# Moving the Newton part of the norm chains to GpSimd, loading the next expert's register earlier, and a new set of due times

## The reference

```
x = x + A(layernorm(x))          # A: linear attention, (theta phi^T) g / 16, no softmax
x = x + F(layernorm(x))          # F: a transformer layer of its own
F(x): h = rmsnorm(x) * ln1;  q, k, v = h @ wqkv   (16 query heads, 4 kv heads of 16), rope on q, k
      x = x + softmax(causal(q k^T / 4)) v @ wo
      h = rmsnorm(x) * ln2;  top 2 of 8 experts by softmax(h @ gate)
      out = sum over chosen experts of weight * (silu(h @ w1) * (h @ w3)) @ w2     (ffn 512)
      return x + out
```

## Time and profile before

| | us |
|---|---|
| median of 3 runs | 1060.29 (1058.63 to 1061.31) |
| the profiled execution, its time | 1058.78 |
| the profiled execution, its span | 1057.1 |
| PE busy | 1011.6 in 6264 instructions |
| DVE busy | 789.2 in 1701 |
| ACT busy | 661.5 in 1305 |
| POOL busy | 435.5 in 476 |
| PE matmuls of `warm` steps (L2046), part of PE busy | 27.5 |

### The profile page before, as it was taken

How to read it: one execution, slowest core, us unless ns; L and a number is a source line. 1 busy time by engine, 2 the same in 40 slices (tenths; PEclk the granted TensorE clock), 3 DMA queues, 4 the chain that set the end, 5 groups by cost and what they waited for, 6 DMA issues and landing times.

```text
span 1057.1 us, 19430 instructions
## 1 busy us (share of the span) xinstructions
PE 1011.6 (96%) x6264; PEld 594.6 (56%) x6264; DVE 789.2 (75%) x1701; ACT 661.5 (63%) x1305; POOL 435.5 (41%) x476
## 2 busy tenths in 40 slices
PE   5999999999999999999999999999989999999997
PEld 4765335443453333453334444456678888888886
DVE  5689979787778998899857997136776666666664
ACT  3562785747768878847767656684534555555553
POOL 1020145155732144422545325457477543444443
PEclk9999999999999999999999999999999999999999
DMA  6433114132336557732343412243434333222220
GB/s 200 128 123 103 53 46 143 55 115 77 97 109 194 146 188 212 203 95 82 111 120 109 137 25 70 52 92 82 103 78 98 73 57 52 48 47 46 48 46 11
DMA packets 86642, 102.33 MB, mean 97 GB/s; under 512 B 17904, under 2 KB 74224, under 8 KB 86544
## 3 DMA queue, kind: packets, MB, share of 16 engines
q1 hardware_dynamic: 72240, 81.46, 26.3%
q0 software_dynamic: 14304, 19.63, 10.1%
HBM read 56.22 MB, written 41.01 MB: 92 GB/s over the span
## 4 chain that ended last, share of the span: by engine, by line
PE 74%; DVE 16%; ACT 5%; issue 3%; DMA 1%; POOL 1%; DVEq 0%; ACTq 0%; POOLq 0%
PE psum L2171 10%; PE psum L2157 9%; PE psum L2209 6%; PE psum L2213 5%; PE psum L2137 5%; PE psum L2210 5%; DVE psum L1932 5%; PE psum L2211 5%; PE psum L2123 3%; PE psum L2219 3%; PE psum L2237 3%; PE psum L2140 2%; PE psum L2231 2%; PE psum L2233 2%; PE psum L2232 2%
## 5 line engine op out<-in xcount | busy, mean ns | idle before, releaser
L1440 ACT ACTIVATE probs_mem<-psum 128x512 f32<-128x512 f32 (+1 forms) x464 | 232.0, 584 | 90.2 <-PE psum L2157 89.0
L1932 DVE CUSTOM_DVE_ANT_1 psum<-psum,masking 128x640 f32<-128x640 f32 (+3 forms) x256 | 257.2, 1045 | 32.9 <-PE psum L2140 32.1
L1337 POOL DMA_INDIRECT out<-yout,labels x71 | 133.7, 1884 | 182.9 <-DMA out<-yout,labels 86.8
L2157 PE MATMUL psum<-stack_mem 98*128 98x512 bf16 (+3 forms) x768 | 169.3, 327 | 3.3 <-DVE mx L1932 1.8
L1292 POOL TENSOR_SCALAR_AFFINE_SELECT probs_mem<-probs_mem 128x512 f32<-128x512 f32 x104 | 66.9, 644 | 223.9 <-ACT probs_mem L1440 223.6
L2157 PEld LDWEIGHTS psum<-stack_mem 98*128 98x128 bf16 x768 | 64.6, 97 | 105.3 <-issue 21.9
L2171 PE MATMUL psum<-probs_mem,v 128*17 128x512 f32 (+3 forms) x1152 | 117.1, 490 | 0.8 <-POOL probs_mem L1292 0.5
L2015 DVE TENSOR_TENSOR w_lo<-w_mem,w_hi 128x1024 fp32r<-128x1024 f32 x51 | 62.5, 1225 | 65.5 <-PE psum L2233 57.3
L1934 DVE TENSOR_REDUCE mx<-psum 128x4 f32<-128x512 f32 (+2 forms) x96 | 96.1, 1036 | 13.1 <-PE psum L2145 10.8
L2137 PE MATMUL psum<-stack_mem 96*128 96x512 bf16 x256 | 95.2, 383 | 5.4 <-DVE mx L1932 2.6
L2209 PE MATMUL psum<-w_hi,x_hi 128*128 x216 | 93.6, 433 | 6.2 <-issue 2.4
(11 more groups left out here) (229 smaller groups left out, 2070.8 us busy)
## 6 DMA issues: line engine op xcount, KB each, us to landing
block<-routed SPq DMA_DIRECT2D x71, 129.0 KB, 2.5
w_mem<-in_w13T SPq DMA_DIRECT2D x16, 512.0 KB, 4.9
qk_parts<-w_mem SPq DMA_DIRECT2D x16, 384.0 KB, 2.9
stack_mem<-qk_parts SPq DMA_DIRECT2D x32, 192.0 KB, 3.3
w_mem<-in_x SPq DMA_DIRECT2D x8, 512.0 KB, 5.1
out<-w_mem SPq DMA_DIRECT2D x8, 512.0 KB, 4.0
x_late<-out SPq DMA_DIRECT2D x8, 512.0 KB, 5.0
stack_mem<-qk_parts SPq DMA_DIRECT2D x32, 128.0 KB, 2.7
```

The costliest lines, as they stand in the source:

```text
L1337: e.indirect_dma_start(out_rows, bass.IndirectOffsetOnAxis(ap=labels[w % NLABEL].bitcast(I32)[:, 0:1], axis=0), youts[w % NYOUT], None, bo ...
L1440: e.activation(probs[probs_of(m)][:, hh:hh + n, q0:CH], grid(turn[step][0][:, 0:n * (CH - q0)], n), ACT.Exp, scale=float(HD) ** -0.5).then ...
L1932: e.tensor_tensor_reduce(keys, keys, masked(w), 1.0, -3e38, ALU.add, ALU.max, to).then_inc(sem["max"], 1)
L2157: m = e.matmul(bk[:, i * (CH - q0):(i + 1) * (CH - q0)], s[0:STACK + NMAX, kt // TPR, GRP, kt % TPR * P:(kt % TPR + 1) * P], s[0:STACK + N ...
```

## The change

Three edits.

1. `rsqrt` is cut in two. The seed is now one DVE instruction in place of two. For batches 1 to 3 norm1 and norm2 stop after the seed on DVE (2 and 3 steps), and norm3 does so for all batches (2 steps); the Newton steps and what follows them run on POOL in chains of 15, 18 and 13 steps (`norm1_rest`, `norm2_rest`, `norm3_rest`). Batch 0's norm1 and norm2 stay on DVE whole. [...]
2. PE's load of the next block's register stands in the second half of the current block's `up`, behind the products of k = 0. The first block of each batch's list (w = 0, 9, 25, 41) still loads ahead of its first half.
3. The planner's costs for `label`, `w2_lo` and the norm steps, its constants `LIKE` and `AHEAD`, and the whole table `NUDGE` are new.

```
-RSQRT_STEPS = 11
+RSQRT_STEPS = 10
-NORM1_STEPS, NORM2_STEPS, NORM3_STEPS = RSQRT_STEPS + 2, RSQRT_STEPS + 5, RSQRT_STEPS + 1
+NORM1_STEPS, NORM2_STEPS, NORM3_STEPS = RSQRT_STEPS + 2, RSQRT_STEPS + 5, 15
+NORM1_SEED, NORM2_SEED, NORM3_SEED = 2, 3, 2
+NORM1_REST, NORM2_REST, NORM3_REST = 15, 18, 13
-TURN, LIKE = 0.1, (3.1, 0.06)
+TURN, LIKE = 0.1, (2.5, 0.05)
-AHEAD = {"DVE": 1.7, "ACT": 1.9}
+AHEAD = {"DVE": 1.9, "ACT": 1.8}
 NUDGE = {
-        "aggr": {(0,): -126.5},
+        "aggr": {(1,): 1.2, (2,): 24.8},
...
+            def newton(name, dst, a, u, w):
+                in_chain(name)
+                e.tensor_scalar(a, a, -0.5, None, ALU.mult).then_inc(sem[name], 1)
+                yield
+                for _ in range(3):
+                    in_chain(name)
+                    e.tensor_tensor(u, dst, dst, ALU.mult).then_inc(sem[name], 1)
+                    yield
+                    in_chain(name)
+                    e.tensor_tensor(w, u, a, ALU.mult).then_inc(sem[name], 1)
+                    yield
+                    in_chain(name)
+                    e.tensor_scalar(w, w, 1.5, None, ALU.add).then_inc(sem[name], 1)
+                    yield
+                    in_chain(name)
+                    e.tensor_tensor(dst, dst, w, ALU.mult).then_inc(sem[name], 1)
+                    yield
...
                 elif stage == "h2":
-                    q.wait_ge("norm3", NORM3_STEPS * (b + 1))
+                    q.wait_ge("norm3_rest", NORM3_REST * (b + 1))
...
-                e.tensor_scalar(ui, ai, 1, None, ALU.logical_shift_right).then_inc(sem[name], 1)
-                yield
-                in_chain(name)
-                e.tensor_scalar(di, ui, -1.0, float(0x5F3759DF), ALU.mult, ALU.add).then_inc(sem[name], 1)
+                e.tensor_scalar(dst.bitcast(I32), a.bitcast(I32), -0.5, float(0x5F3759DF), ALU.mult, ALU.add).then_inc(sem[name], 1)
...
                 elif stage == "gate":
-                    q.wait_ge("norm3", NORM3_STEPS * (b + 1))
+                    q.wait_ge("norm3_rest", NORM3_REST * (b + 1))
...
-                    if half == 0:
+                    if half == 0 and w not in offset:
...
                             m = e.matmul(bk, blockT[w % 2][:, k], w13_s[:, k, of], start=first, stop=final)
+                        if half == 1 and first and (gi, c + 1) in WORK:
+                            offset[w + 1] = e.value_load(bexp[gi][0:1, c + 1:c + 2], min_val=0, max_val=(NE - 1) * 2 * FFN)
```

More of the change, by code:

```diff
@@ L246, in work_of @@
         return ("PE", 1.38 if at[0] >= DOWN_FROM else 1.73), ("ACT", 0.37), ("POOL", 1.6)
+    if stage in ("norm1", "norm2", "norm3"):
+        seed = {"norm1": NORM1_SEED, "norm2": NORM2_SEED, "norm3": NORM3_SEED}[stage]
+        return (("POOL", 0.2),) if at[1] >= seed and (at[0] or stage == "norm3") else (("DVE", 0.08),)
     if stage == "w13_lo":
@@ L288 @@
+        "split": {(3,): 9.6},
+        "spread": {(3,): 6.6},
+        "square": {(1,): 0.7},
+        "square_sum": {(2,): -9.6},
+        "stats": {(3,): 5.8},
+        "stats2": {(1,): 9.4, (2,): 0.3},
+        "theta": {(2,): 55.7, (3,): -46.6},
+        "v": {(1,): -9, (2,): -90.5, (3,): -1.2},
+        "w13": {(): -75.5},
+        "weight": {(0,): 48},
+        "wo": {(2,): -37.3},
+        "x1": {(2,): -5.4},
+        "xn": {(1,): 23.3},
+        "xnT": {(1,): -0.5, (3,): -1.2},
 }
@@ L377, in needs @@
         if stage == "norm2":
-            return [("aggr2", b, (TPB if b else HALF * (at[1] // NORM2_STEPS + 1)) - 1)] + [(stage, b, at[1] - 1)] * (at[1] > 0) + [(stage, b - 1, norm_parts(b - 1) * NORM2_STEPS - 1)] * (b > 0 and not at[1])
+            return [("aggr2", b, (TPB if b else HALF * (at[1] // NORM2_STEPS + 1)) - 1)] + [(stage, b, at[1] - 1)] * (at[1] > 0) + [(stage, b - 1, norm_parts(b - 1) * norm_steps("norm2", b - 1) - 1)] * (b > 0 and not at[1])
         if stage == "h":
-            return [("norm2", b, (1 if b else at[1] // HALF + 1) * NORM2_STEPS - 1)] + in_order(step)
+            return [("norm2", b, (1 if b else at[1] // HALF + 1) * norm_steps("norm2", b) - 1)] + in_order(step)
         if stage == "hT":
@@ L538, in project @@
                 continue
-            steps += [(half, ("norm1", b, i)) for i in one_part(b, half, NORM1_STEPS)] + [(half, ("xn", b, j)) for j in (range(TPB) if b else tiles)]
+            steps += [(half, ("norm1", b, i)) for i in one_part(b, half, norm_steps("norm1", b))] + [(half, ("xn", b, j)) for j in (range(TPB) if b else tiles)]
         steps += [(2, ("gram", b, i)) for i in range(gram_steps(b))] + [(2, ("square", b, i)) for i in range(2)]
@@ L548, in project @@
                 continue
-            steps += [(6 + half, ("norm2", b, i)) for i in one_part(b, half, NORM2_STEPS)]
+            steps += [(6 + half, ("norm2", b, i)) for i in one_part(b, half, norm_steps("norm2", b))]
             for at in range(2) if b else (half,):
@@ L948, in mega_kernel, with normed @@
         routing = [carve(route_mem, route_sizes)] * len(GROUPS)
+        def normed(stage, b, n):
+            if b < 1:
+                return stage, {"norm1": NORM1_STEPS, "norm2": NORM2_STEPS}[stage] * n * (b == 0)
+            return f"{stage}_rest", {"norm1": NORM1_REST, "norm2": NORM2_REST}[stage] * b
         def masked(w):
@@ L1269, in _, with norm3_rest, go_on @@
+            def norm3_rest(b):
+                q.wait_ge("norm3", NORM3_SEED * (b + 1))
+                t = rt[:, 2]
+                yield from newton("norm3_rest", rstd2, t[:, 1], t[:, 2], t[:, 3])
+            def go_on(make, b):
+                if (make, b) not in chains:
+                    chains[make, b] = make(b)
+                next(chains[make, b])
             for step in orders["POOL"]:
                 stage, *at = step
-                if stage == "split":
+                if stage == "norm1":
+                    go_on(norm1_rest, at[0])
+                elif stage == "norm2":
+                    go_on(norm2_rest, at[0])
+                elif stage == "norm3":
+                    go_on(norm3_rest, at[0])
+                elif stage == "split":
@@ L1567, in norm2 @@
                     yield
-                    yield from rsqrt("norm2", scale, s[:, 0:2], s[:, 2:4], s[:, 4:6])
+                    seed("norm2", scale, s[:, 0:2])
+                    yield
+                    if b:
+                        return
+                    yield from newton("norm2", scale, s[:, 0:2], s[:, 2:4], s[:, 4:6])
                     in_chain("norm2")
@@ L1583, in norm3 @@
                 q.wait_ge("h2", TPB * b)
+                q.wait_ge("norm3_rest", NORM3_REST * b)
                 t = rt[:, 2]
@@ L1587, in norm3 @@
                 yield
-                yield from rsqrt("norm3", rstd2, t[:, 1], t[:, 2], t[:, 3])
+                seed("norm3", rstd2, t[:, 1])
+                yield
             def route(gi):
```

116 lines of the change are left out of this document (78 added, 38 removed), and 2 rows, old and new, of the table WORK_OF.

## The result

The changed kernel takes 1042.05 us, the median of four runs (1039.46 to 1044.08), against 1059.6 for the kernel before beside it. The ratio is 0.983, with a 95% interval of 0.981 to 0.986. The forecast was 1044.

A forecast was written before the change was run, and what follows sets the result against it. Up to 800 us PE had 62 us of slack; after that PE or its sequencer bound the kernel. 9 (load, last stage) + 2 (earlier blocks) + 5 (chains, order) = 16 us off 1058.78, plus 1.5: 1044, range 1031 to 1056.

The forecast's parts named there:

- the largest term: Last stage, from 800 us on: moving the register load off the block border gains 9 us.
- the last step of the sum: Whole kernel: the median lies 1.5 us above the profiled execution, turning 1042.8 into 1044.3 us.
- The last stage: 9 forecast: Expert blocks from w = 23 on: 9 us gained, the middle of 11.5 by PE and 6.4 by the adds.
- a lead of 1.5 us: Second half of `up`: PE's sequencer is 1.5 us ahead, covering some 0.6 us of load, so it costs nothing.
- PE's 11.5: Last stage by PE alone: 46 moved loads at 0.25 us each gain 11.5 us.
- the adds' 6.4: Last stage if an add into `out` takes 5.03 us each: 46 x 0.14 = 6.4 us gained.
- an upper figure of the adds' period: Adds into `out`: 5.03 us each is above a free-running chain's floor, since issues take 1.56 to 2.16 us.
- The chains and the order with the blocks up to w = 22: 7 forecast: Stretch up to 800 us: shorter by some 7 us, 2 from blocks w = 13 to 22 and 5 from chains and order.
- The 5 us for chains and order: Norm chains and new order together: 5 us, half of 9.3 us of removed filler; possibly nothing, minus 6 or 15.
- The rival of late chains: Norm chains queue on POOL, steps 0.8 us, `h` 10 to 12 us late: 1073, slower than before; chance 0.10.
- The signs: Marks of being right: no PEld idle at block starts, period 4.9 to 5.05 us, DVE down 20, POOL up 30.

The follow-up runs named there:

- the kernel with less PE work: The changed kernel without the product w_lo x x_hi in `up` from w = 23 on, so part of the result is missing: 1027.79 us (0.970).
- the later copy: The changed kernel with the copy of batch 3's second routing weights moved behind the w_lo of down(22) in DVE's queue: 1039.24 us (0.979).
- the old due times and the order kept: The load-only kernel with the Newton parts run on POOL where DVE's steps stood in planner time, all other orders kept: 1054.36 us (0.995).
- with the old due times a part of it did: The changed kernel with the old NUDGE, LIKE, AHEAD and costs, so edits 1 and 2 without 3: 1060.9 us (1.000).
- the kernel with the old load: The changed kernel with edit 2 undone, the register load back at the border between blocks: 1054.74 us (0.996).
- 23 fillers: The later-copy kernel plus 23 filler matmuls on PE ahead of five steps that follow idle time: 1035.86 us (0.978).
- the kernel with the load alone: The kernel before with edit 2 only, the next block's register loaded in mid-block: 1044.73 us (0.985).
- POOL's queue was mended: The kernel with fillers, batch 3's scatters spread between the adds and the weight copy behind the x_lo of block 25: 1032.66 us (0.975).

## Why the prediction was right

The time was right within 2 us, and so was the mechanism of the largest term. Two sizes were off in opposite directions, 3.0 us too little and 4.4 us too much, and nearly cancelled: that the time came out so close is in part luck. So is the last step of the sum, which set the median 1.5 us above the profiled execution; after, it was 2 us below.

**The last stage: 9 forecast, 12.0 measured.** Both inputs held: 0.25 us a block for the load (0.67 against 0.92 us, periods 0.26 us apart) and a lead of 1.5 us (two loads covered, four not). The sum has 46 moved loads where the 46 periods hold 44, which the 0.27 us of each makes up for. The term that was mis-sized is the middle that I took between PE's 11.5 and the adds' 6.4. I held 5.03 us for an upper figure of the adds' period and still let it take 2.5 us from the sum. The adds at 4.67 us in the kernel with less PE work show that they were no bound at 4.91. But my reason for calling 5.03 us an upper figure, issues of up to 2.16 us, was wrong too. The six adds from 879.10 on all had short issues; two of them:

```profile
884.27 1.56 POOL L1337 DMA_INDIRECT out<-yout,labels  x1 [3.41 <-DMA out<-yout,labels]
...
904.65 1.56 POOL L1337 DMA_INDIRECT out<-yout,labels  x1 [3.21 <-issue]
```

They came 5.03 us apart although each started 1.4 to 2.2 us behind its result, so that only the add before held it back. From w = 25 to 66 the same distance is 4.90 us in the changed kernel, 4.88 with the later copy and 4.71 with less PE work, with most issues at 1.55 us in all three. What makes the landing of the add before come sooner in one kernel than in the other is open, and the earlier trace rows alone could not have told it.

**The chains and the order with the blocks up to w = 22: 7 forecast, 2.6 measured.** The 5 us for chains and order were a guess at half of a sum, and the runs show what stands behind the small number: minus 16 and plus 19 us, by the two edits in turn. I costed the chains at nothing, also at `norm3_rest(3)`; measured with the old due times and the order kept, they cost 9.6 us, mostly at `norm1(2)` and `norm2(3)`. The rival of late chains had the mechanism, POOL's queue, and the wrong reason: the steps are 0.30 us apart and not 0.8, but they stand among splits of 1.15 us, and one chain step took 1.70 us. In the changed kernel that rival did not come; with the old due times a part of it did. From the trace before alone this could not be told, and I gave it 0.10.

**The clock.** The sum has no term for PE's clock, and it fell in three new places. It would be easy to blame the 34 `warm` steps that are gone, and the runs do not bear that out. Half of them stood from 440 to 480 us (18 steps before, 1 after), where the clock stayed full. Ahead of the three places there are more of them than before: 5 against 3 from 60 to 100 us, 1 against none from 480 to 490. And the kernel with the old load has the same 67 steps and falls in only one of the three. What is shown is that 23 fillers in the idle stretches ahead of the three places keep the clock up there. How much a low clock costs is not measured by itself; in the five runs of the kernel with the later copy 7.5 us lie between the one with the lowest clock and the one with the highest.

**The signs.** Right: the idle time ahead of L2209 is gone, the period is 4.9 us, the adds wait for each other with issues of 1.56 us, DVE is down by 21.3 us of busy time (20 forecast). The chain steps start 0.28 to 0.34 us apart, not 0.25. POOL rose by 19.2 us and not by 30: 151 steps of some 0.22 us are 33 us, and the adds gave 15 back, since their issue got shorter, 71 times from 1884 to 1676 ns (the page's group of the adds, after, below). The stretch up to 800 us is shorter by 2.6 us and not 7.

```profile
L1449 POOL DMA_INDIRECT out<-yout,labels x71 | 119.0, 1676 | 179.2 <-DMA out<-yout,labels 118.4
```

The kernel with the load alone gains 15.1 us by the median and the changed kernel 17.5, so nearly everything that was asked of three edits came from the smallest one.

## What to carry to other kernels

A register load in the instruction stream of a busy engine costs the engine time unless the sequencer is ahead of it; put the load where the sequencer is ahead, and measure the lead by adding loads until they cost. A set of due times is fitted to one set of steps, so an edit that moves steps has to be judged with its own table too, and the same edit with its order kept shows what the move costs in that order. A wait in an engine's strict queue holds up all that stands behind it, and when PE is freed of it, look at once at the queue that ends the kernel: here PE gained 6 us and the end 2, until POOL's queue was mended too.

## What the runs showed of the hardware

- In the changed kernel PE's granted clock fell to 1.2 GHz for 3.4 or 6.8 us around idle stretches of 1.5 to 4.3 us, and not to the same extent in every execution of one kernel (mean 0.990 to 0.995 of full speed in five runs of the kernel with the later copy).
- The load of the next block's register takes 0.64 us of PE's sequencer. It cost 0.25 us of PE time at the border of two blocks and nothing in the middle of one, where the sequencer is some 1.5 us ahead. Three loads more cost 0.82 us.
- An add's issue takes 1.55 us by itself. In the kernel before, from w = 22 on, it was 1.75 to 2.46 us for the 35 adds that ran beside DVE's `w_lo` for over 0.3 us, and 1.55 to 1.73 us for the 14 others.
- Adds into `out` that wait for nothing but the landing of the one before come every 4.88 us in one kernel whose results come every 4.90, and every 4.71 in another whose results come every 4.68. That the two keep so close together, with a lag of 7 us in the one and 3 to 5 in the other, is not explained by any run here.
- A small elementwise step of a chain takes 0.30 us on POOL and 0.20 us on DVE, start to start, and both engines show single steps of 1 to 1.7 us among them (and 66.30 above).
